# The self-attention's preparation taken batch by batch, inside the attention loops on either side of it

## The chip, the core and the metric

The kernel runs on one core of a Trainium2 chip. The time is device microseconds (us) of one launch. The core has a matrix engine (PE in the profile; its weight loads, which overlap the products, are PEld), a vector engine (DVE), a scalar engine (ACT), a general engine (POOL) and a sync engine (SP) that issues the transfers. Each engine works through its own instructions in the order in which the program gives them; between engines there are only semaphores.

## The reference

Four decoder layers on `x` of 2 batches x 256 tokens x 128 channels. The last layer is a cross attention with 16 heads of 64 over 512 context rows, and then a block whose first part is this (16 query heads, 4 key and value heads of 8 channels, causal):

```python
x = x + xattn3(layernorm(x), ctx, mask_k, ...)
h = rmsnorm(layernorm(x), ln1_w)
qkv = h @ wqkv.T
q, k, v = split(qkv)
q, k = rope(q), rope(k)
x = layernorm(x) + causal_attention(q, k, v) @ wo.T
x = x + moe(rmsnorm(x))
```

The two batches are independent of one another in all of it. What a kernel must give back is `x` after the last mixture of experts (8 experts, 2 chosen per token).

## The kernel before, in words

One launch does all layers; activations stay on the chip. The order on every engine is written out by hand: each engine has one function, in it loops with small helpers, and a helper that is called at some `n`, `step` or `part` of a loop stands there in that engine's queue.

The last cross attention (`attention3`) runs over 32 pairs `n` (two heads, one half of a batch's queries; batch 0 is n = 0 to 15). PE does the scores of pair n (`scores_pair`, L1903), VectorE the maxima (L1031), ScalarE the exponentials (L663), VectorE the scaling by the sums (`scale_pair`, L1014, one pair behind), PE the transposes (`turn_pair`, L1914, two pairs behind), ScalarE copies them (L655), and at every odd n PE multiplies half a group of four heads with the values (`values_part`, L1929). VectorE copies a finished group out (`out3`, L1020). `project3(0)` and `project3(1)` (L1966) are the output projections of the batches; both stand at the end of the loop.

Then all that the self-attention needs is prepared for both batches at once, with nothing beside it: the residual, two norms whose roots are taken on POOL (L1456 to L1475, L471 to L484), a transpose (L1571), its copy (L556), the projection to queries, keys and values (L2267), the rotation (L1489 to L1496), a split of each number into three bf16 parts (`split`, L912 to L916), their spreading into a table `REP` (`spread`, L317, one part each on POOL, ScalarE and VectorE) of 8 tiles (keys and queries of 4 token tiles), 80 transposes of it (`stack`, L1620) in 12 lots, and a copy of each lot to where the attention reads it (`stack_copy`, L302, even lots on VectorE, odd ones on ScalarE). `keep_busy` (L1989) puts 10 products whose result nobody reads into two waits of PE:

```python
keep_busy(7, 5)
turn_xn(9)
...
keep_busy(3, 7)
stack(ROPE_TILES)
stacked(pe, ROPE_TILES[-1])
```

The self-attention (`attention_self` on PE, `attention(2)` on ScalarE and VectorE) runs over 8 groups `g` of four heads (batch 0 is g = 0 to 3) in 12 steps, each of which holds four stages of different groups: the maxima of the scores of group `step` (three banks: PE L1635 to L1644, VectorE L926 and L929), their split and transpose (VectorE L996 to L1000, PE L1764), the scores again with the maxima taken off (L1660 to L1675) and the exponentials (L614) of group `step - 2`, the products with the values (L1783, L1786) of `step - 3`, and the transpose back (L1806) of `step - 4`. The mixture of experts follows (L1869, L1881).

## Time and profile before

| | us |
|---|---|
| three runs | 560.18, 559.19, 559.20 |
| median | 559.20 |
| span of the profiled execution, first to last instruction | 557.4 |
| PE busy in the span | 503.7 (90%) |
| VectorE busy | 354.4 (64%) |
| ScalarE busy | 312.1 (56%) |
| POOL busy | 62.5 (11%) |

The profiled execution has no time of its own in the list beside its span; the median lies 1.8 us above the span, and that is taken as what lies around it. A row of the profile names an instruction by engine, source line and tile: `L1914 PE ps<-const_t,Qst` is line 1914, run on PE, written to `ps` (the accumulators) from `const_t` and `Qst`. In rows of time the first number is the start in the span and the second how long the merged instructions took; what stands in brackets at the end is the idle time before them and what ended it. The granted clock of PE is given as a share of its full speed: 1.00 is 2.4 GHz and 0.50 is 1.2 GHz.

### The profile page before, as it was taken

Reading aid. Unit: us, or ns where it says so; the run is one execution under the profiler, and the core shown is the slowest. Engines: PE = TensorE matmul, PEld = TensorE weight load, DVE = VectorE, ACT = ScalarE, POOL = GpSimd, SP = SyncE. Lnnn points to the kernel's source line nnn. Section 1 sums busy time; section 2 is a strip of 40 time slices with the busy share of each in tenths; the row PEclk is TensorE's granted clock in tenths of the full one; section 3 lists DMA queues with packets and bytes.
Section 4 is the critical chain, followed back from the end, with each engine's and each line's share of the span. In section 5 each row is a group of like instructions: output and inputs, shape, how many; then the busy total and the mean of one; then the engine's idle time right before and its main releaser. Section 6 shows DMA issues by size and latency. Waiting matters only on the chain.

```text
span 557.4 us, 9259 instructions
## 1 busy us (share of the span) xinstructions
PE 503.7 (90%) x3340; PEld 308.6 (55%) x3344; DVE 354.4 (64%) x922; ACT 312.1 (56%) x537; POOL 62.5 (11%) x161
## 2 busy tenths in 40 slices
PE   5889998999979998898887699999999868988997
PEld 2334456999924444445553234555557545556987
DVE  6767746565888772496336656787773486554664
ACT  6447786463326776148357289788783043555331
POOL 4021120100011110000270000000001230000000
PEclk9889999999989999899998799999999987999999
DMA  4669301034224000000000000000000500000000
GB/s 142 198 183 405 123 4 34 2 86 132 76 74 149 1 1 1 2 0 1 1 0 1 1 0 1 1 1 2 1 2 0 228 0 1 1 2 1 2 11 10
DMA packets 11612, 26.17 MB, mean 47 GB/s; under 512 B 2128, under 2 KB 6864, under 8 KB 10928
## 3 DMA queue, kind: packets, MB, share of 16 engines
q1 hardware_dynamic: 11568, 25.59, 13.9%
q8 instruction: 27, 0.44, 0.3%
q14 instruction: 17, 0.14, 0.1%
HBM read 22.44 MB, written 3.15 MB: 46 GB/s over the span
## 4 chain that ended last, share of the span: by engine, by line
PE 75%; DVE 10%; ACT 5%; issue 4%; DMA 2%; SPq 2%; POOL 1%; DVEq 0%; ACTq 0%; POOLq 0%
PE ps L1903 6%; PE ps L1914 6%; PE ps L1929 5%; PE ps L2020 5%; PE ps L2008 5%; PE ps L1707 5%; PE ps L1791 5%; PE ps L1869 4%; PE ps L1689 4%; DVE mxs L924 3%; PE ps L1979 2%; PE ps L1881 2%; PE ps L2167 2%; PE ps L1989 2%; PE ps L1718 1%
## 5 line engine op out<-in xcount | busy, mean ns | idle before, releaser
L924 DVE TENSOR_REDUCE mxs<-ps 128x1 f32<-128x512 f32 x128 | 81.8, 682 | 23.9 <-PE ps L1707 22.5
L614 ACT ACTIVATE PR<-ps 128x1024 f32<-128x1024 f32 x80 | 77.4, 977 | 34.9 <-PE ps L1689 17.4
L1031 DVE TENSOR_REDUCE nm<-ps 128x1 f32<-128x512 f32 x64 | 41.1, 684 | 25.0 <-PE ps L1903 25.0
L1707 PE MATMUL ps<-Kst,Qst 84*128 84x512 bf16 x128 | 49.8, 398 | 6.3 <-DVE mxs L924 3.4
L655 ACT COPY PR<-ps 128x512 f32<-128x512 f32 x64 | 37.9, 596 | 16.9 <-PE ps L1914 16.9
L663 ACT ACTIVATE Qst<-ps,nm 128x512 f32<-128x512 f32 x64 | 45.5, 710 | 1.5 <-DVE nm L1031 1.3
L1689 PE MATMUL ps<-Qst,Kst 84*128 84x256 bf16 x256 | 45.8, 273 | 0.1
L1914 PEld LDWEIGHTS ps<-const_t,Qst 128*128 128x128 f32 x256 | 27.4, 140 | 24.3 <-DVE Qst L1014 11.8
L692 ACT ACTIVATE PR<-ps,cols_t 128x256 f32<-128x256 f32 x64 | 26.5, 471 | 23.4 <-PE ps L2008 23.0
L623 ACT COPY Qst<-ps 12x1024 bf16<-12x1024 bf16 x24 | 24.0, 999 | 27.6 <-PE ps L1764 27.6
L1903 PE MATMUL ps<-VX,FC 64*128 64x512 f32 x128 | 36.1, 641 | 0.1
L1914 PE MATMUL ps<-const_t,Qst 128*128 128x128 f32 x256 | 35.4, 280 | 0.9 <-ACT PR L655 0.9
L1791 PE MATMUL ps<-PR,VX 128*9 128x256 f32 x512 | 33.5, 380 | 0.0
L2020 PEld LDWEIGHTS ps<-FC,PR 128*128 128x128 f32 x256 | 30.9, 192 | 0.8
L1707 PEld LDWEIGHTS ps<-Kst,Qst 84*128 84x128 bf16 x128 | 12.7, 100 | 33.6 <-DVE mxs L924 22.6
L1689 PEld LDWEIGHTS ps<-Qst,Kst 84*128 84x128 bf16 x256 | 23.3, 97 | 14.4 <-issue 2.3
L2008 PE MATMUL ps<-parts,FC 128*128 128x256 f32 x128 | 30.4, 381 | 0.9 <-DVE scr L974 0.8
L1869 PE MATMUL ps<-scr,FC 128*128 128x256 f32 x128 | 30.6, 382 | 0.6 <-DVE scr L974 0.6
L2020 PE MATMUL ps<-FC,PR 128*128 128x128 f32 x256 | 31.0, 275 | 0.0
L1929 PE MATMUL ps<-PR,Kst 128*64 128x256 f32 x256 | 30.9, 385 | 0.0
L1014 DVE TENSOR_SCALAR Qst<-Qst,rsum 128x512 f32<-128x512 f32 x64 | 28.3, 484 | 1.1
L1989 PE MATMUL ps<-ctxT,const_t 128*128 128x512 f32 x48 | 23.6, 640 | 5.7 <-DMA const_t<-in_const 5.7
(369 smaller groups left out, 883.5 us busy)
## 6 DMA issues: line engine op xcount, KB each, us to landing
Kst<-k_rows SPq DMA_DIRECT2D x48, 96.0 KB
FC<-in_fc SPq DMA_DIRECT2D x2, 2048.0 KB, 12.0
Qst<-q_rows SPq DMA_DIRECT2D x48, 48.0 KB
FC<-in_w SPq DMA_DIRECT2D x1, 2048.0 KB, 8.7
k_rows<-REP SPq DMA_DIRECT2D x12, 128.0 KB, 2.2
REP<-in_w SPq DMA_DIRECT2D x1, 1536.0 KB, 6.8
q_rows<-REP SPq DMA_DIRECT2D x20, 64.0 KB, 2.0
FC<-in_w2e SPq DMA_DIRECT2D x1, 1024.0 KB, 10.8
```

What stands on the lines that cost most here:

```text
L614: act.activation(PRg[:, g % 2, u * 1024:u * 1024 + width], bank(3 + 2 * (n % 2), 2)[:, 0:width], ACT.Exp, scale=scale).then_inc(s.p_ready, 1)
L663: act.activation(P3[:, i % 8, :], bank(S_BANKS[n % 2][half]), ACT.Exp, bias=nm3[:, i % 8:i % 8 + 1], accum_out=sum3[:, i % 16:i % 16 + 1]) ...
L924: i = dve.tensor_reduce(m[:, u // 4, u % 4:u % 4 + 1], bank(n % 2), AX_X, ALU.max)
L1689: i = pe.matmul(bank(3 + 2 * (n % 2), 2)[:, k * SQ:(k + 1) * SQ], Kst[0:ROWS_A, b, h0 + u, k * P:(k + 1) * P], Qst[0:ROWS_A, b, h0 + u, :] ...
L1707: pe.matmul(bank(n % 2), Qst[0:ROWS_A, b, h, q0:q0 + P], Kst[0:ROWS_A, b, h, :], start=True, stop=True).then_inc(s.smax_ready, 1)
L1791: i = pe.matmul(o[32 * c:32 * c + HD + 1, :], Vaug[:, 4 * b + k, h0 + c, 0:HD + 1], pr[:, c * 1024 + k * SQ:c * 1024 + (k + 1) * SQ], star ...
L1869: i = pe.matmul(bank(2 * (n % 2) + c // 2)[:, c % 2 * SQ:(c % 2 + 1) * SQ], w13[:, e, c * P:(c + 1) * P], lnT[:, b * SQ:(b + 1) * SQ], sta ...
L1903: pe.matmul(bank(S_BANKS[n % 2][half]), Q3[d0:d0 + DH3, r, q0:q0 + P], K3[d0:d0 + DH3, r, b * SK:(b + 1) * SK], start=True, stop=True)\
L1914: ins = pe.transpose(bank(T_BANKS[half])[:, k * P:(k + 1) * P], P3[:, i % 8, k * P:(k + 1) * P], ident)
L1929: pv = pe.matmul(bank(O_BANKS[g % 2])[DH3 * c:DH3 * (c + 1), r * SQ:(r + 1) * SQ], V3[:, 4 * b + k, DH3 * (h0 + 2 * r + c):DH3 * (h0 + 2 * ...
L2008: i = pe.matmul(bank(2 * (n % 2) + c // 2)[:, c % 2 * SQ:(c % 2 + 1) * SQ], fc1[:, n % E, c * P:(c + 1) * P], hdT[:, n % 3, :], start=True ...
L2020: i = pe.matmul(bank(4 + n % 2)[:, j * P:(j + 1) * P], actT[:, n % 2, c, j * P:(j + 1) * P], fc2[:, n % E, c, :], start=(c == 0), stop=(c ...
```

## The change

The preparation is cut by batch. Batch 0's is put into the second half of `attention3` (pairs 22 to 35): its projection into bank 7 at n = 22 on PE, the residual and norms on VectorE at n = 23 to 25, transposes at 26, their copy on ScalarE at 27, the projection at 28, the rotation on VectorE at 29, the split and all spreading on POOL alone, and 40 transposes in two pieces among the last value products. Bank 7 is free for this since the groups 4 to 7 all gather their output in bank 6. Batch 1's is put into the first steps of the self-attention: its projection in step 0, the norms at the ends of steps 0 and 1 and in step 2, projection in step 2, rotation, split and a third of the spreading on VectorE at the start of step 3 (the other two thirds on POOL), and 40 transposes on PE ahead of step 4, the first step that works on batch 1's scores. `keep_busy` is gone from here. Batch 0's queries and the rotation's tables move into the storage of the values that groups 0 to 3 have used up.

The first piece is PE's queue at the end of the cross attention, before the change: L1929 are value products, L1966 the projections, L1989 `keep_busy`, L1571 and L2267 the transposes and projection, L1620 the transposes of the table, L1635 the first scores of the self-attention.

```order
L1914 MATMUL ps<-const_t,Qst 128x128 x16
L1929 MATMUL ps<-PR,Kst 64x256 x8
L1966 MATMUL ps<-wd_t,REP 128x128 x16
L1929 MATMUL ps<-PR,Kst 64x256 x16
L1966 MATMUL ps<-wd_t,scr 128x128 x16
L1989 MATMUL ps<-ctxT,const_t 128x512 x7
L1571 MATMUL ps<-const_t,xn 128x128 x4
L2267 MATMUL ps<-wd_t,scr 128x192 x4
L1989 MATMUL ps<-ctxT,const_t 128x512 x3
L1620 MATMUL ps<-identb,REP 96x128 x80
L1635 MATMUL ps<-FC,Qst 128x128
```

The same place after the change; here L1993 are the value products, L1666 the transposes of the table, L1689 and L1691 the first scores of the self-attention and their mask, L2037 the projection of batch 1, L1696 the next scores.

```order
L1978 MATMUL ps<-const_t,Qst 128x128 x16
L1993 MATMUL ps<-PR,Kst 64x256 x8
L1666 MATMUL ps<-identb,REP 96x128 x20
L1993 MATMUL ps<-PR,Kst 64x256 x8
L1666 MATMUL ps<-identb,REP 96x128 x20
L1993 MATMUL ps<-PR,Kst 64x256 x8
L1689 MATMUL ps<-FC,Kst 128x128
L1691 MATMUL ps<-maskb,identb 128x128
L2037 MATMUL ps<-wd_t,scr 128x128 x16
L1696 MATMUL ps<-FC,Kst 128x256
```

The projection of batch 0 has left this place for n = 22; the one of batch 1 has moved behind the first scores; 40 of the 80 transposes stand between the value products, and the other 40 have gone further down, ahead of step 4.

The second piece is VectorE's queue in the first steps of the self-attention, before (L926 and L929 read the maxima of a step, L996 to L1000 split them):

```order
L302 COPY Qst<-ps 96x8x128 x2
L926 TENSOR_REDUCE mxs<-ps 128x4
L929 TENSOR_REDUCE mxs<-ps 128x2 x2
L996 TENSOR_SCALAR mp<-mxs 128x2x4
L997 SCALAR_TENSOR_TENSOR mr<-mxs,mp 128x8
L999 CAST mp<-mr 128x2x4
L1000 TENSOR_TENSOR mp<-mr,mp 128x2x4
```

The same after, step 0 and the start of step 1 (L995 and L998 are the maxima, L885 to L888 `last_projected(1)`, L1076 to L1080 the split):

```order
L1100 COPY scr<-ps 128x512
L995 TENSOR_REDUCE mxs<-ps 128x4
L998 TENSOR_REDUCE mxs<-ps 128x2 x2
L885 TENSOR_TENSOR x<-x,ps 128x256
L1168 BN_STATS st<-x 128x6 x2
L1171 BN_AGGR mv<-st 128x2 x2
L888 COPY Kst<-x 128x256
L1076 TENSOR_SCALAR mp<-mxs 128x2x4
L1077 SCALAR_TENSOR_TENSOR mr<-mxs,mp 128x8
L1079 CAST mp<-mr 128x2x4
L1080 TENSOR_TENSOR mp<-mr,mp 128x2x4
```

And after, the end of step 2 and the start of step 3 (L922 and L926 end the rotation of batch 1, L981 to L985 its split, L321 the spreading):

```order
L1080 TENSOR_TENSOR mp<-mr,mp 128x2x4
L919 TENSOR_TENSOR Kst<-ps,const_t 128x160
L920 TENSOR_TENSOR Kst<-ps,const_t 128x20x4
L921 TENSOR_TENSOR Kst<-ps,const_t 128x20x4
L922 COPY FC<-ps 128x4x8
```

```order
L926 TENSOR_TENSOR Kst<-Kst 128x320
L981 CAST parts<-Kst 128x320
L982 TENSOR_TENSOR rest<-Kst,parts 128x320
L983 CAST parts<-rest 128x320
L984 TENSOR_TENSOR rest<-rest,parts 128x320
L985 CAST parts<-rest 128x320
L321 COPY REP<-parts 128x4x3x8
L321 COPY REP<-parts 128x16x24
L321 COPY REP<-parts 128x4x3x8
L321 COPY REP<-parts 128x16x24
L995 TENSOR_REDUCE mxs<-ps 128x4
```

What VectorE had done before the self-attention began now stands between the maxima of step 0 and their split, and in front of the maxima of step 3.

```diff
+        Qs4 = [Kst[:, 0, 0:8, :].rearrange("p g (a t) -> p (g a) t", a=2), Qst[:, 1, :, :]]
...
-        ROPE_TILES = range(0, 8)
+        ROPE_TILES = (range(0, 4), range(4, 8))
+        LOT_BANKS = (0, 1, 2, 3, 0, 1, 6, 0, 1, 6, 0, 1)
+        LOT_BEHIND = (None, None, None, None, 0, 1, None, None, None, 6, 7, 8)
...
+        def o3_bank(g):
+            return O_BANKS[g % 2] if g < G // 2 else O_BANKS[0]
...
-            pool.wait_ge(s.proj_ready, 4)
+            rstd_of(8, 0, of_batch(0))
+            rstd_after(9, 0, of_batch(0))
+            link(pool.memset(V4[:, :, :, :], 0.0))
+            pool.memset(V4[:, :, :, HD:HD + 1], 1.0).then_inc(s.setup_pool, 1)
             pool.memset(REP[:, :].bitcast(F32), 0.0).then_inc(s.setup_pool, 1)
-            pool.wait_ge(s.setup_pool, 4)
-            rstd_of(8)
-            rstd_after(9)
-            for n in ROPE_TILES:
-                spread(pool, n)
+            pool.wait_ge(s.setup_pool, 5)
+            pool.wait_ge(s.rope_ready, 1)
+            ropes, r = qrope[:, 0:2, :].rearrange("p t n -> p (t n)"), rest[:, 0:320]
+            link(pool.tensor_copy(parts[:, 0, 0:320], ropes))
+            link(pool.tensor_tensor(r, ropes, parts[:, 0, 0:320], ALU.subtract))
+            link(pool.tensor_copy(parts[:, 1, 0:320], r))
+            link(pool.tensor_tensor(r, r, parts[:, 1, 0:320], ALU.subtract))
+            link(pool.tensor_copy(parts[:, 2, 0:320], r))
+            for n in ROPE_TILES[0]:
+                for j in range(NPART):
+                    i = spread(pool, n, j)
+                    if j < NPART - 1:
+                        link(i)
+                i.then_inc(s.rep_first, 1)
+            rstd_of(8, 1, of_batch(1))
+            rstd_after(9, 1, of_batch(1))
+            for n in ROPE_TILES[1]:
+                for j in range(2):
+                    pool.wait_ge(s.parts_ready, j + 1)
+                    if j == 0:
+                        pool.wait_ge(s.rep_turned, lots_till[n - 4])
+                    spread(pool, n, j).then_inc(s.rep_pool, 1)
...
+            def rms1_out(b, at):
+                act.wait_ge(s.xn_turned, TURNS.index((9, b)) + 1)
+                act.activation(rms1T[b], at[:, 0:SQ], ACT.Copy, scale=CB["rms1"]).then_inc(s.lnT_ready, 1)
...
+                    if a == 2 and step == G // 2:
+                        stack_lots(act, ROPE_TILES[1])
...
+                        if a == 2 and step == 2 and part == 0:
+                            rms1_out(1, bank(6))
...
+                    if n == 27:
+                        rms1_out(0, bank(7))
...
-            ln_out(9)
-            act.wait_ge(s.setup_pool, 4)
-            spread_and_stack(act, ROPE_TILES, ROPE_TILES)
+            stack_lots(act, ROPE_TILES[0])
...
+            def last_projected(b, at):
+                dve.wait_ge(s.proj_ready, 4 + b)
+                link(dve.tensor_tensor(x[:, of_batch(b), :], x[:, of_batch(b), :],
+                                       at[:, 0:SQ].rearrange("p (t n) -> p t n", t=2), ALU.add))
+                batch_variances(b)
+                link(dve.tensor_copy(kept[:, b * SQ:(b + 1) * SQ].rearrange("p (t n) -> p t n", t=2),
+                                     x[:, of_batch(b), :]))
+            def last_normalised(b):
+                dve.wait_ge(s.rstd_ready, norm(8, b) + 1)
+                for t in (2 * b, 2 * b + 1):
+                    i = dve.tensor_scalar(x[:, t, :], x[:, t, :], mv[:, t, 0:1], rstd[:, t:t + 1],
+                                          ALU.subtract, ALU.mult)
+                signal_xn(i, norm(8, b) + 1)
+            def last_scaled(b):
+                dve.wait_ge(s.rstd_ready, norm(9, b) + 1)
+                for t in (2 * b, 2 * b + 1):
+                    i = dve.tensor_scalar(xn[:, t, :], x[:, t, :], rstd[:, NT + t:NT + t + 1], None, ALU.mult)
+                i.then_inc(s.xn_ready, 1)
+            def ropes(b, at):
+                dve.wait_ge(s.qkv_ready, b + 1)
...
+                q2 = qrope[:, 2 * b:2 * b + 2, :]
+                signal(dve.tensor_tensor(q2, q2, qrot[:, 2 * b:2 * b + 2, :], ALU.add), 'rope_ready')
+            def last_spreads():
+                split(qrope[:, 2:4, :].rearrange("p t n -> p (t n)"), 320, 320)
+                for n in ROPE_TILES[1]:
+                    dve.wait_ge(s.rep_turned, lots_till[n - 4])
+                    spread(dve, n, 2).then_inc(s.rep_dve, 1)
...
+                    if a == 2 and step == 3:
+                        ropes(1, bank(6))
+                        last_spreads()
+                    if a == 2 and step == G // 2:
+                        stack_lots(dve, ROPE_TILES[1])
...
+                        if a == 2 and step == 0 and part == 7:
+                            last_projected(1, bank(6))
+                        if a == 2 and step == 1 and part == 7:
+                            last_normalised(1)
+                        if a == 2 and step == 2 and part == 1:
+                            last_scaled(1)
...
-                for n in range(PAIRS3 + PV3 + 4):
+                for n in range(4 * G + PV3 + 1):
+                    g, part = divmod(n - PV3 - 4, 4)
+                    if 0 <= g < G and part == 0:
+                        out3(g)
                     if n < PAIRS3:
                         for half in range(2):
                             i = 2 * n + half
                                               negate=True).then_inc(s.nm3_ready, 1)
                     if 0 <= n - 1 < PAIRS3:
                         scale_pair(n - 1)
-                    g, part = divmod(n - PV3 - 4, 4)
-                    if 0 <= g < G and part == 0:
-                        out3(g)
+                    if n == 23:
+                        last_projected(0, bank(7))
+                    if n == 24:
+                        last_normalised(0)
+                    if n == 25:
+                        last_scaled(0)
+                    if n == 29:
+                        dve.wait_ge(s.setup_pool, 5)
+                        ropes(0, bank(7))
+                    if n == PAIRS3 + 3:
+                        stack_lots(dve, ROPE_TILES[0])
...
-                    for spread_by in (s.rep_dve, s.rep_act, s.rep_pool):
-                        pe.wait_ge(spread_by, tl + 1)
-                    if n >= 4:
-                        pe.wait_ge(s.stack_act if n % 2 else s.stack_dve, (n - 4) // 2 + 1)
+                    if tl < 4:
+                        pe.wait_ge(s.rep_first, tl + 1)
+                    else:
+                        pe.wait_ge(s.rep_pool, 2 * (tl - 4) + 2)
+                        pe.wait_ge(s.rep_dve, tl - 4 + 1)
+                    behind = LOT_BEHIND[n]
+                    if behind is not None:
+                        pe.wait_ge(s.stack_act if behind % 2 else s.stack_dve, behind // 2 + 1)
...
+            def qkv(b, at):
+                pe.wait_ge(s.lnT_ready, rows_copied(9, b))
+                for j in range(2):
+                    i = pe.matmul(at[:, 192 * j:192 * (j + 1)], rms1T[b][:, j * P:(j + 1) * P],
+                                  WD["wqkv"], start=True, stop=True)
+                i.then_inc(s.qkv_ready, 1)
...
+                    if step == G // 2:
+                        pe.wait_ge(s.smax_read, MAXB[a] + 3 * step)
+                        stack(ROPE_TILES[1])
+                        stacked(pe, ROPE_TILES[1][-1])
                     for part in range(4):
                         if step < G:
                             scores_max(a, step, part)
+                        if step == 0 and part == 1:
+                            project3(1)
+                        if step == 2 and part == 0:
+                            turn_rows(9, 1, bank(6))
+                        if step == 2 and part == 3:
+                            qkv(1, bank(6))
...
-                            pe.wait_ge(s.o3_ready, g - 1)
+                            pe.wait_ge(s.o3_ready, g if g > G // 2 else g - 1)
...
-                    if n == PAIRS3 + LAG:
-                        project3(0)
                     if n >= PV3 and (n - PV3) % 2:
                         values_part(*divmod(n - PV3 - 1, 4))
                         values_part(*divmod(n - PV3, 4))
+                    if n == 22:
+                        project3(0)
+                    if n == 26:
+                        turn_rows(9, 0, bank(7))
+                    if n == 28:
+                        qkv(0, bank(7))
+                    if n == PAIRS3 + 1:
+                        stack(ROPE_TILES[0][0:2])
+                    if n == PAIRS3 + 3:
+                        stack(ROPE_TILES[0][2:4])
...
-                pe.wait_ge(s.p3_ready, 2 * PAIRS3 - 2)
                 pe.wait_ge(s.o3_ready, G // 2 * (b + 1))
                 for t in (2 * b, 2 * b + 1):
                     for r in range(8):
-                        i = pe.matmul(bank(1 - b)[:, t % 2 * P:(t % 2 + 1) * P],
+                        i = pe.matmul(bank(7 - b)[:, t % 2 * P:(t % 2 + 1) * P],
...
-            project3(1)
-            keep_busy(7, 5)
-            turn_xn(9)
-            pe.wait_ge(s.lnT_ready, 10)
...
-            keep_busy(3, 7)
-            stack(ROPE_TILES)
-            stacked(pe, ROPE_TILES[-1])
+            stacked(pe, ROPE_TILES[0][-1])
```

## Rows read from the trace of the kernel before

**Rows 1.** Busy us of each engine by stretch; PEclk is the granted clock.
```profile
345.00:420.00 75.00, 74.92 (x498) 41.67 (x500) 57.01 (x129) 59.39 (x150) 0.00 (x0) 1.00 0.01 1
...
437.00:462.50 25.50, 18.45 (x112) 12.44 (x110) 16.72 (x60) 8.22 (x15) 7.47 (x14) 0.87 0.18 73
462.50:477.90 15.40, 13.82 (x114) 8.48 (x114) 10.53 (x28) 6.51 (x8) 0.00 (x0) 0.78 0.01 1
```
**Rows 2.** Timeline: PE where the cross attention ends; first transposes back.
```profile
424.83 3.84 PE L1966 MATMUL ps<-wd_t,REP 128*128 128x128 f32 x32
428.60 3.67 PE L1929 MATMUL ps<-PR,Kst 128*64 128x256 f32 x32
...
433.16 3.81 PE L1966 MATMUL ps<-wd_t,scr 128*128 128x128 f32 x32 [0.89 <-DVE scr L1020]
...
477.95 0.41 PE L1806 MATMUL ps<-const_t,scr 128*128 128x128 f32 x2 [0.64 <-issue]
```
**Rows 3.** Timeline of the cross attention: VectorE, and PE's transposes of a pair.
```profile
403.40 1.29 DVE L1031 TENSOR_REDUCE nm<-ps 128x1 f32<-128x512 f32 x2 [1.61 <-PE ps L1903]
...
405.59 0.68 DVE L1020 COPY scr<-ps 128x512 f32<-128x512 f32 x1
...
410.88 0.88 DVE L1014 TENSOR_SCALAR Qst<-Qst,rsum 128x512 f32<-128x512 f32 x2
...
411.46 1.13 PE L1914 MATMUL ps<-const_t,Qst 128*128 128x128 f32 x8
...
413.06 0.88 DVE L1014 TENSOR_SCALAR Qst<-Qst,rsum 128x512 f32<-128x512 f32 x2
```
**Rows 4.** Timeline of the preparation: VectorE.
```profile
437.00 0.42 DVE L1456 TENSOR_TENSOR x<-x,ps 128x256 f32<-128x256 f32 x1 [3.15 <-PE ps L1966]
...
438.28 0.39 DVE L1470 COPY scr<-x 128x512 f32<-128x512 f32 x1
...
439.98 1.12 DVE L862 TENSOR_SCALAR x<-x,mv,rstd 128x128 f32<-128x128 f32 x4 [1.31 <-POOL rstd L472]
...
445.41 0.33 DVE L1489 TENSOR_TENSOR PR<-ps,const_t 128x160 f32<-128x160 f32 x1 [1.76 <-PE ps L2267]
...
447.31 0.33 DVE L912 CAST parts<-PR 128x320 bf16<-128x320 f32 x1
...
449.73 0.70 DVE L317 COPY REP<-parts 128x96 bf16<-128x96 bf16 x4
```
**Rows 5.** Timeline of the preparation: PE.
```profile
444.45 1.57 PE L2267 MATMUL ps<-wd_t,scr 128*128 128x192 f32 x8 [0.78 <-ACT scr L556]
...
450.05 1.54 PE L1620 MATMUL ps<-identb,REP 128*96 128x128 bf16 x24 [1.46 <-DVE REP L317]
...
455.26 6.14 PE L1620 MATMUL ps<-identb,REP 128*96 128x128 bf16 x56 [3.67 <-DVE FC L302]
```
**Rows 6.** Groups of POOL by form: busy us, mean ns, idle before.
```profile
L317 POOL COPY REP<-parts 128x384 bf16<-128x384 bf16 x4 | 2.5, 615 | 3.0 <-PE ps L1620 3.0
...
L524 POOL TENSOR_SCALAR PR<-PR 128x352 f32<-128x352 f32 x1 | 1.4, 1395 | 0.1
```
**Rows 7.** Timeline of POOL in the preparation.
```profile
447.70 2.25 POOL L317 COPY REP<-parts 128x96 bf16<-128x96 bf16 x4 [5.72 <-DVE parts L912]
...
457.31 0.51 POOL L317 COPY REP<-parts 128x384 bf16<-128x384 bf16 x1 [3.03 <-PE ps L1620]
```
**Rows 8.** Busy us by stretch, around a fall of the clock.
```profile
450.90:454.30 3.40, 0.69 (x13) 0.54 (x10) 3.19 (x12) 1.83 (x4) 1.66 (x3) 1.00 0.00 0
454.30:461.10 6.80, 5.84 (x55) 5.87 (x56) 4.02 (x11) 3.43 (x6) 0.51 (x1) 0.51 0.01 2
```
**Rows 9.** Timeline of the self-attention's start: PE, VectorE, ScalarE.
```profile
461.44 1.01 ACT L302 COPY Qst<-ps 96x1024 bf16<-96x1024 bf16 x1 [1.08 <-PE ps L1620]
...
463.82 1.38 DVE L929 TENSOR_REDUCE mxs<-ps 128x2 f32<-128x512 f32 x2
465.23 0.17 DVE L996 TENSOR_SCALAR mp<-mxs 128x8 bf16<-128x8 f32 x1
...
468.41 0.64 PE L1660 MATMUL ps<-Qst,FC 96*128 96x512 bf16 x1
...
470.54 0.42 PE L1642 MATMUL ps<-FC,Qst 96*128 96x256 bf16 x1
...
470.79 1.02 ACT L614 ACTIVATE PR<-ps 128x1024 f32<-128x1024 f32 x1 [3.26 <-PE ps L1665]
```

More of the change, by code:

```diff
@@ L316, in spread, with stack_lots @@
                 .to_broadcast([P, heads, 3, HD])
-            i = eng.copy(to, src) if eng is nc.scalar else eng.tensor_copy(to, src)
-            i.then_inc(done, 1)
-        def spread_and_stack(eng, to_spread, to_stack):
+            return eng.tensor_copy(to, src)
+        def stack_lots(eng, tile_range):
             odd, done = (1, s.stack_act) if eng is nc.scalar else (0, s.stack_dve)
-            def stack_lots(tile):
-                for n, (tl, h0, nh) in enumerate(lots):
-                    if tl == tile and n % 2 == odd:
-                        eng.wait_ge(s.rep_turned, n + 1)
-                        stack_copy(eng, n, tl, h0, nh).then_inc(done, 1)
-            behind = list(to_stack)
-            for n in to_spread:
-                spread(eng, n)
-                while behind and behind[0] <= n - 2:
-                    stack_lots(behind.pop(0))
-            for tile in behind:
-                stack_lots(tile)
+            for n, (tl, h0, nh) in enumerate(lots):
+                if tl in tile_range and n % 2 == odd:
+                    eng.wait_ge(s.rep_turned, n + 1)
+                    stack_copy(eng, n, tl, h0, nh).then_inc(done, 1)
         MROW0 = [0, 0, PAD]
@@ L1501, in _ @@
-            spread_and_stack(dve, ROPE_TILES[4:8], ROPE_TILES)
             def route_logits(b):
```

142 lines of the change are left out of this document (51 added, 91 removed).

## The prediction

> **What bounds the kernel now.** I read the shares of busy time first: PE 90% against 64% for VectorE, so PE sets the time wherever it is full. Then the busy time by stretch, to see where it is full. In the cross attention it is: 74.92 of 75.00 us at full clock, with VectorE at 57.01 and ScalarE at 59.39 [rows 1]. In the preparation it is not: 18.45 of 25.50 us at a mean clock of 0.87, and 6.17 of those were `keep_busy`; and in the first steps of the self-attention PE is busy 13.82 of 15.40 us, but at 0.78 of its clock [rows 1]. Last the timeline of both stretches: PE waits there for VectorE (3.67 us ahead of the last 56 transposes, 1.46 ahead of the first 24 [rows 5]), which works through a chain (residual, norm, norm, rotation, split, spread) with PE, POOL and ScalarE as links [rows 4].
>
> The part that the change touches runs from the end of the last but one group's value products (424.83) to the first transpose back (477.95 [rows 2]): 53.1 us, low stretches of the clock included. The profiled execution took 557.4 us by its span; the median is 559.2, so 1.8 lies around the span. I rebuild these 53.1 us for the new order, with what is put into the loop added.
>
> **The change part by part.** At full clock:
>
> 1. Into the loop. `project3(0)` moves, 3.84 [rows 2] wherever it stands. Two transposes of batch 0 at 0.14 each (8 in 1.13 [rows 3]) are 0.3, its projection is half of 1.57 [rows 5]: 0.8. PE is full there, so all of it counts. VectorE's insertions count where they delay PE. The smallest rows hide: between reduces VectorE idles 1.61 in a pair [rows 3], and the residual with its statistics (437.00 to 438.67, less half a copy for half the tokens: 1.4), the normalising (half of 1.12) and the scaling (0.6 at most) [rows 4] fit in it. The rotation does not: 445.41 to 447.31, 1.9 [rows 4], and `out3` with 0.68 [rows 3] now stands ahead of the reduces. 1.9 + 0.6 less 1.61 and less the 0.14 by which the scaling ends (410.88 + 0.44) before its transposes start at 411.46 leaves 0.8 late. Together 5.7 (4.9 if the delay is caught up; 7.0 if neither gap can be used).
> 2. 40 transposes of batch 0, 0.055 each (1.54 for 24 less the start-up [rows 5]): 2.2, and the last group's values 3.67 [rows 2]: 5.9.
> 3. The wait for `out3` (0.89) and `project3(1)` (3.81) [rows 2]: 4.7. The first scores go ahead of it.
> 4. From there VectorE has what the preparation had, now in the middle of the maxima: 0.5 for scores, five reads at 0.69 (two in 1.38 [rows 9]) 3.4, residual and statistics 1.4, two splits of maxima 1.4 (465.23 to 465.93 each [rows 9]), two half sets of scalings 1.1 [rows 4], and 0.5 for semaphores. That is 8.3, with PE mostly idle. What is queued behind the waiting VectorE is the split of step 0's maxima, for which PE's mask transposes and ScalarE's copy wait in turn.
> 5. Step 2 up to the projection of batch 1: transposes 0.3, the exponentials' products (468.41 to 470.54 at half clock [rows 9], so 1.1), ScalarE's exponential 1.02 [rows 9] ahead of its copy of half the 0.78 [rows 5] (0.4), some scores 0.5, projection 0.8: 4.1. The copy waits on ScalarE for PE, and the next mask copy and exponentials queue behind it.
> 6. VectorE's rotation, split and spreads of batch 1, 445.41 to 450.43: 5.0 [rows 4]. They stand ahead of step 3's maxima, so every stage behind waits; with a maxima read (0.69) and what is left of a split (0.5) 6.2. A third of the spreads, the split and the rotation were on this path before; the two thirds of the spreading that POOL does are eight at 0.56 (four in 2.25 [rows 7]), 4.5 beside VectorE's split and spreads, so hidden.
> 7. What is left of step 3 on PE: one set of exponentials' products at full clock and a third of one: 1.4.
> 8. 40 transposes of batch 1 ahead of step 4: 2.2, and the later of their 6 lots wait for a copy before them out of three banks, on ScalarE 1.01 each [rows 9]: 3.9 (2.2 if no copy is waited for, 4.2 if two on ScalarE are).
>
> The sum is 5.7 + 5.9 + 4.7 + 8.3 + 4.1 + 6.2 + 1.4 + 3.9 = 40.2, against 53.1: 12.9 saved.
>
> The clock takes some back. PE's clock fell to its lower level (0.51, which is 1.2 GHz) for 6.80 us after PE had been busy 0.69 of 3.40 us [rows 8]. Of before's two such stretches in the interval the new order keeps the cause: parts 4 and 6 leave PE idle for several us, with no `keep_busy` between. So I expect two stretches of some 6.8 us; full of work one costs half, 3.4, and with VectorE's chain in it as little as nothing. I take 2.0 and 1.8, the middle: 12.9 - 3.8 = 9.1 saved, and 557.4 - 9.1 + 1.8 = 550.0 us (rounded).
>
> POOL's new chain has to hide. Its five split operations on 320 columns have no row of before: the nearest are 1.40 (352 columns of 32 bits, one input [rows 6]) and 0.51 (384 columns of 16 bits [rows 7]). I take 0.7, nearer to the second, since three of the five write bf16. 3.5 + twelve spreads at 0.56 [rows 7] 6.7 + 17 links at 0.08 (estimate from the gaps between spreads) 1.4 = 11.6. The rotation stands behind the scalings at 413.06 [rows 3] and ends 0.9 + 1.9 later, at 415.9; PE comes to the last tile's transposes at 424.83 + 1.1 (20 transposes) + 1.84 (half the last values) + 0.2 (4 more) + 0.8 (the delay of part 1) = 428.8, 12.9 later: hidden by 1.3. With 1.40 for each split operation and 0.615 for a spread [rows 6] it is 15.8, and PE waits 2.9.
>
> The row has POOL's spread at 0.56 beside a working VectorE and 0.51 alone [rows 7]. The Trainium skill (GPSIMD Engine Reference, § 3.1 Elementwise, side-by-side cycle accounting) speaks against the move of the two subtractions: it has POOL at about half VectorE's rate for two inputs, 4497 ns for 2048 columns, an estimate of 0.7 us for 320; with 0.7 the sum would stay as it is, by the upper row it loses the 2.9.
>
> The loads of the experts' weights that wait for the end of the cross attention start some 4 us later and are wanted first 40 us behind: hidden. The clearing of the table and of the values moves onto a POOL that is idle in the loop (0.00 of 75 [rows 1]).
>
> **The rivals.** *The clock holds* (0.25): one low stretch, or two that lie beside VectorE's chain and cost 1.0 in all. For it: PE has work put between part 4 and 6. Against: the 0.69 of 3.40 that came before the fall. 557.4 - 11.9 + 1.8 = 547.3.
>
> *POOL's split is slow* (0.12): 1.40 each as above; PE waits 2.9 ahead of the last transposes and a low clock of 1.1 more follows: 554.0.
>
> *POOL is held up by VectorE, and the kernel is slower* (0.08). VectorE is busy 57 of 75 us in the loop [rows 1], and no row shows a POOL copy beside its scaling. If POOL's operations take f times as long, batch 0 is late by 10.2f - 11.5 and batch 1 by 4.5f - 6.3 (its spreads against the 5.0 of part 6 and the first 24 transposes): 14.7f - 17.8 in all. It decides at f = 1.8; at f = 2 the loss is 11.6 and the time 561.6, 2.4 slower than before. Against it stand the 0.56 and 0.51 of rows 7.
> The Trainium skill has such a rule (GPSIMD Engine Reference, § 1 Specifications): POOL shares its SBUF interfaces with VectorE and contends with instructions that use both ports or two SBUF inputs. By that rule the spreads beside the split of VectorE should have suffered too, and the trace's 10% does not agree with a factor of 2.
>
> *VectorE becomes the bound of the loop* (0.07): it works 57 of 75 us, and if each of the ten pairs from n = 23 on comes 0.8 late, 8 of the 9.1 are lost: 558.2. Against: its idle 1.61 comes in each pair [rows 3].
>
> **How the numbers follow.** The forecast has 0.48, with a range of its own of 547.5 to 552.5 (clock 1.4 to 6.3 in place of 3.8, and part 1 from 4.9 to 7.0). The range goes from 546.5 (the clock holds, and the transposes' copies hide) to 555.0 (slow split): 0.85 of the cases less their edges. A measurement of this kernel tells 0.2%, 1.1 us, from no change. Faster: the first three cases, 0.85, and one in seven of the last, 0.86. Same: the rest of the last, 0.06. Slower: 0.08.
>
> **What the profile after would show.** Right: the value products of the last groups run on with transposes between them without a wait for POOL; the first scores of the self-attention come some 12 us after the start of the last group; PE's idle time ends on VectorE's maxima in steps 0, 1 and 3, in all about 12 us; two stretches of PEclk near 0.5 between step 1 and step 4; from the second half of the self-attention on, every row is as before, 9 us earlier. Wrong: idle PE ahead of the 40 transposes ended by POOL; in pairs 23 to 33 idle PE ended by VectorE on more than one or two pairs; steps 4 and later at other intervals than before; a wait for the experts' weights; or a chain of waits that runs through POOL in step 3.

## The result, and the profile after

The changed kernel took 551.78, 549.03, 553.14 and 553.74 us, median 552.5, beside 559.2 for the kernel before: a ratio of 0.9871, 95% interval 0.9834 to 0.9909. A second set on another occasion gave a median of 552.5 in five executions (a sixth took 1782 us and is left out) and 0.9872 (0.9816 to 0.9928); the medians by themselves differ by 6.7 us in the first set and by 5.2 in the second (557.7 before). The forecast was 550.0 in 546.5 to 555.0, faster. The profiled execution of the changed kernel has a span of 549.9 us, against 557.4.

PE's timeline at the end of the cross attention and in the first steps, after. The lines are the answer to [rows 2, 5]; line numbers are those of the changed kernel (L1978 the transposes of a pair, L1666 those of the table, L1993 the value products, L1689 the first scores, L2037 the projection of batch 1, L1818 the transposes of the maxima, L1620 those of batch 1, L1674 its projection, L1860 the first transpose back).

```profile
410.67 1.09 PE L1978 MATMUL ps<-const_t,Qst 128*128 128x128 f32 x8 [0.80 <-DVE Qst L1094]
...
424.70 1.24 PE L1978 MATMUL ps<-const_t,Qst 128*128 128x128 f32 x8 [1.23 <-DVE Qst L1094]
...
429.18 1.12 PE L1978 MATMUL ps<-const_t,Qst 128*128 128x128 f32 x8 [0.33 <-ACT PR L678]
...
432.10 1.32 PE L1666 MATMUL ps<-identb,REP 128*96 128x128 bf16 x20
433.35 1.95 PE L1993 MATMUL ps<-PR,Kst 128*64 128x256 f32 x16
435.23 1.32 PE L1666 MATMUL ps<-identb,REP 128*96 128x128 bf16 x20
...
438.35 0.23 PE L1689 MATMUL ps<-FC,Kst 96*128 96x128 bf16 x1
...
439.21 3.84 PE L2037 MATMUL ps<-wd_t,scr 128*128 128x128 f32 x32 [0.22 <-DVE scr L1100]
442.89 0.27 PE L1696 MATMUL ps<-FC,Kst 96*128 96x256 bf16 x1
...
446.92 0.28 PE L1818 MATMUL ps<-identb,mp 128*12 128x128 bf16 x2 [1.63 <-DVE mp L1080]
...
450.53 0.69 PE L1620 MATMUL ps<-const_t,xn 128*128 128x128 f32 x2 [2.50 <-DVE xn L903]
...
455.68 0.92 PE L1674 MATMUL ps<-wd_t,scr 128*128 128x192 f32 x4 [0.19 <-ACT scr L576]
456.43 0.38 PE L1724 MATMUL ps<-Kst,FC 96*128 96x512 bf16 x1
...
462.82 0.37 PE L1696 MATMUL ps<-FC,Kst 96*128 96x256 bf16 x1 [2.77 <-DVE mxs L995]
...
465.41 3.93 PE L1666 MATMUL ps<-identb,REP 128*96 128x128 bf16 x40
470.49 0.41 PE L1860 MATMUL ps<-const_t,scr 128*128 128x128 f32 x2 [1.15 <-DVE Qst L311]
```

The preparation's own stretch of 25.5 us [rows 1] is gone. What is left of its waits for VectorE stands in the steps: 1.63, 2.50 and 2.77 us, one each in steps 1, 2 and 3, where the forecast had named steps 0, 1 and 3. (From 440 to 472 us PE is busy 23.0 of 32.0 us, so it idles 9.0, where the forecast said about 12.) The value products run on with transposes between them, and no wait of PE in this stretch ends on POOL.

The busy time by stretch of the same kernel (length, then PE, PEld, DVE, ACT, POOL, and the granted clock), as in [rows 1, 8]:

```profile
345.00:420.00 75.00, 73.56 (x499) 42.88 (x498) 57.44 (x132) 55.95 (x141) 5.81 (x9) 1.00 0.01 1
447.99:454.80 6.81, 4.31 (x24) 2.92 (x24) 3.03 (x11) 0.80 (x2) 0.65 (x1) 0.50 0.01 2
454.80:461.80 7.00, 5.06 (x47) 3.12 (x46) 6.54 (x23) 4.45 (x6) 2.27 (x4) 0.99 0.00 0
461.80:468.60 6.80, 5.78 (x48) 4.41 (x49) 3.95 (x11) 2.33 (x4) 1.51 (x5) 0.51 0.00 0
```

Two stretches of 6.8 us at the lower level (1.2 GHz), each beginning in one of the long waits above, with full clock between them. And PE, which had been full in the cross attention (74.92 of 75.00), is now at 73.56: 0.53 of that is a wait for ScalarE that the kernel before has as well, just ahead of 345.00; most of the rest is the wait of 0.80 above, which is new.

**The interval that is compared below.** The first value products of the cross attention start between 344.2 and 348.6 us, differing from trace to trace of kernels that have the same instructions up to there, and from the first transpose back in step 4 to the end every trace has 79.4 us. So each trace is read from its first value products to that transpose, in two parts: the cross attention (to the end of its last value products) and the rest.

| trace | cross attention | from there to the first transpose back | sum |
|---|---|---|---|
| before, two traces | 86.63, 86.59 | 45.68, 44.31 | 132.31, 130.90 |
| after, two traces | 92.27, 92.27 | 32.07, 32.86 | 124.34, 125.13 |

### The profile page after: what moved, and what is told of

It is laid out like the page before. It is cut to its first block, busy times and chain, and to the rows that moved or that the text cites. A ratio compares the mean times of both kernels' runs of the same rounds, so it can differ in the third digit from the quotient of the medians.

```text
span 549.9 us, 9205 instructions
## 1 busy us (share of the span) xinstructions
PE 491.1 (89%) x3320; PEld 302.8 (55%) x3324; DVE 354.1 (64%) x912; ACT 309.8 (56%) x530; POOL 72.7 (13%) x186
## 4 chain that ended last, share of the span: by engine, by line
PE 71%; DVE 14%; issue 5%; ACT 5%; SPq 2%; DMA 2%; POOL 1%; DVEq 0%; ACTq 0%; POOLq 0%
PE ps L2091 5%; PE ps L2079 5%; PE ps L1761 5%; PE ps L1967 5%; PE ps L1978 5%; PE ps L1845 5%; PE ps L1993 5%; PE ps L1933 4%; PE ps L1743 4%; DVE mxs L993 3%; PE ps L2050 2%; PE ps L1945 2%; PE ps L1860 1%; PE ps L1772 1%; PE ps L2037 1%
## 5 line engine op out<-in xcount | busy, mean ns | idle before, releaser
L468 POOL TENSOR_SCALAR ve<-mv 128x2 f32<-128x2 f32 (+1 forms) x13 | 3.0, 233 | 306.5 <-DVE mv L1171 169.3
L1978 PEld LDWEIGHTS ps<-const_t,Qst 128*128 128x128 f32 x256 | 27.5, 140 | 26.6 <-DVE Qst L1094 14.4
L1978 PE MATMUL ps<-const_t,Qst 128*128 128x128 f32 x256 | 35.4, 280 | 3.0 <-DVE Qst L1094 2.0
L646 ACT COPY Qst<-ps 12x1024 bf16<-12x1024 bf16 x20 | 20.0, 999 | 23.6 <-PE ps L1818 23.6
L1094 DVE TENSOR_SCALAR Qst<-Qst,rsum 128x512 f32<-128x512 f32 x64 | 30.6, 520 | 1.1
L1993 PE MATMUL ps<-PR,Kst 128*64 128x256 f32 x256 | 31.2, 385 | 0.0
```

The source lines that it names most:

```text
L1978: ins = pe.transpose(bank(T_BANKS[half])[:, k * P:(k + 1) * P], P3[:, i % 8, k * P:(k + 1) * P], ident)
L1993: pv = pe.matmul(bank(o3_bank(g))[DH3 * c:DH3 * (c + 1), r * SQ:(r + 1) * SQ], V3[:, 4 * b + k, DH3 * (h0 + 2 * r + c):DH3 * (h0 + 2 * r + ...
```

## The experiments

**The same kernel again.**

> The changed kernel once more, without an edit, to see how its time spreads: its four runs lay between 549.0 and 553.7 us, those of the kernel before within 1.0. Theory (the two low stretches of PE's clock come at another place from run to run, since PE idles for several us where VectorE prepares batch 1): again a spread of 3 to 5 us, median 550 to 553. Rival (the first runs were disturbed): a spread under 1.5 us. In its trace two stretches of 6.8 us at the lower clock between the first scores and the first transpose back.

The five runs lay between 548.15 and 553.0, as the theory has it. But the kernel before, measured beside it, now spread too (556.6 to 565.1 in 17 runs), so the low stretches that are new in the changed kernel are not shown to be the cause. Its two traces differ by 0.8 us in the steps, where the first low stretch fell later in the second; what the other runs differ by has no trace, and the start of the cross attention alone moves by up to 4.4 us from trace to trace. A second trace of the kernel before:

> The kernel before once more, for a second trace of its interval from the first value products to the first transpose back (132.31 us in the first). Theory (the interval depends on where the low clock falls in the preparation, as in the changed kernel): 130 to 133.5, differing from the first by over 0.5. Rival (fixed): 132.2 to 132.4.

132.31 became 130.90 us. In the two traces the mean clock of the preparation and of the first steps was 0.84 and 0.78, then 0.92 and 0.89; it is the clock that differs. So the 53.1 us of the forecast are one trace's. First the first trace, then the second:

```profile
441.00:462.50 21.50, 14.46 (x103) 10.73 (x101) 14.11 (x49) 8.22 (x15) 5.40 (x9) 0.84 0.03 10
462.50:477.90 15.40, 13.82 (x114) 8.48 (x114) 10.53 (x28) 6.51 (x8) 0.00 (x0) 0.78 0.01 1
```

```profile
441.30:463.90 22.60, 15.51 (x109) 10.61 (x108) 15.11 (x52) 8.12 (x15) 7.21 (x13) 0.92 0.12 49
463.90:479.00 15.10, 12.69 (x114) 7.73 (x115) 10.55 (x28) 6.51 (x8) 0.00 (x0) 0.89 0.00 1
```

**Is the low clock worth what was taken for it?** Unread products in PE's three waits, first too many:

```diff
+                            keep_busy(5, 7)
                             turn_rows(9, 1, bank(6))
...
+                        if step == 1 and part == 2:
+                            keep_busy(3, 7)
...
+                        if step == 3 and part == 2:
+                            pe.wait_ge(s.rope_ready, 2)
+                            keep_busy(6, 6)
```

> Products whose result nobody reads are put into PE's three waits for VectorE: three in step 1 ahead of the transposes of the maxima, five in step 2 ahead of the transposes of batch 1, six in step 3 behind the transposes of the maxima. Theory (the low clock costs what the forecast took, 3.8 us): no low stretch there, the projection of batch 1 about 1.8 us earlier against the first scores, step 4's first transpose back 3 to 4 us earlier, time 3 to 4 us below the changed kernel of the same call. Rival (VectorE's chain sets the time of these steps, so a faster PE only waits longer): under 1 us. Second rival: the products run past the end of the waits and cost up to 1 us.

The time stayed (552.1 us, ratio to before 0.9889, 0.9840 to 0.9938). But this does not speak for the rival: the clock was at 1.00 throughout, and the products (L2066) simply ran too long, twice what I had reckoned for one. It is the second rival's case, and dearer than it had it: from the first score to the first transpose back this trace takes 33.10 us, where the changed kernel takes 32.14 and 32.93, so all that the clock gave was lost again.

```profile
444.41 2.79 PE L2066 MATMUL ps<-ctxT,const_t 128*128 128x512 f32 x6
447.69 4.51 PE L2066 MATMUL ps<-ctxT,const_t 128*128 128x512 f32 x10
459.75 5.42 PE L2066 MATMUL ps<-ctxT,const_t 128*128 128x512 f32 x12
```

Three calls show as six products and take 2.79 us where PE had waited 1.63. With 4, 5 and 5 products of half the width in the same places:

> The same three places as in the run with 3, 5 and 6 unread products, where each took 0.88 us, twice what was reckoned, and ran 0.9, 1.7 and 2.3 us past the end of VectorE's work. Now 4, 5 and 5 products of half the width (0.44 each by that run): 1.8, 2.2 and 2.2 us, inside the waits of 1.8, 2.6 and 2.4. Theory (low clock costs what the forecast took): no low stretch, no wait ended by these products, the first score to the first transpose back of step 4 in 28.0 to 29.2 us against 32.1 and 32.9 in the two traces of the changed kernel; time 3 to 4.5 us below it. Rival (VectorE's chain sets the time): 31.5 or more there.

```profile
443.40:451.00 7.60, 6.62 (x46) 4.90 (x44) 6.71 (x23) 1.00 (x1) 2.28 (x6) 1.00 0.58 246
451.00:458.70 7.70, 7.21 (x69) 4.84 (x69) 5.80 (x20) 4.01 (x5) 0.75 (x2) 1.00 0.01 2
458.70:461.20 2.50, 2.40 (x11) 1.79 (x10) 2.43 (x8) 1.00 (x1) 2.50 (x6) 1.00 0.00 0
461.20:467.00 5.80, 4.10 (x59) 3.28 (x60) 3.56 (x9) 3.36 (x5) 0.53 (x2) 1.00 0.00 0
```

548.2 us, ratio 0.9806 (0.9783 to 0.9828). From the first score to the first transpose back 28.24 us against 32.14 and 32.93: the two stretches cost 3.9 and 4.7 us, where the forecast took 3.8. VectorE's chain by itself does not set the time of these steps while the clock is low.

**How much is batch 1's move worth?** Its preparation ahead of the self-attention, batch 0's left in the loop (PE's part; the calls on the other engines move likewise):

```diff
             attention3()
+            project3(1)
             stacked(pe, ROPE_TILES[0][-1])
+            turn_rows(9, 1, bank(6))
+            qkv(1, bank(6))
+            stack(ROPE_TILES[1])
+            stacked(pe, ROPE_TILES[1][-1])
```

> Batch 1's preparation is taken out of the self-attention's steps and put ahead of them, with nothing beside it; batch 0's stays inside the cross attention. Theory: from the end of the cross attention's values the chain of batch 1 is the projection 3.9, residual 1.3, roots on POOL 2.8, scaling, transposes, copy and projection 2.4, rotation 1.9, split 2.2, spreads 0.6, transposes 3.5 and copies 1.0, some 20 us, and then the first four steps as before the change 15.4, so 35 to 36 against 32.1 in the changed kernel: 3 to 4 us slower than it, and still 3 to 5 faster than the kernel before, which is what batch 0 alone is worth. Rival (what batch 1's work hides in the steps it takes from them again, so only batch 0's move counts): within 1 us of the changed kernel.

> The kernel with batch 1's preparation ahead of the self-attention once more. Its interval was 129.97 us in the trace, 2.3 below the kernel before, while its times were level with it (ratio 1.0009). Theory (the traced run was its fastest, and the low clock falls worse in the others): an interval of 131 to 133. Rival (the interval is fixed and the difference lies ahead of it): 129.9 to 130.1, with times again level because its early stages are slower.

558.7 and 558.6 us, ratios to before 1.0009 (0.9993 to 1.0025) and 0.9993 (0.9964 to 1.0022): with batch 0 alone moved the times show no gain, and the changed kernel is 6 us faster than this one. I had expected 3 to 5 for batch 0 alone; that is refuted. The chain of one batch is shorter than that of two, but by less than half: from the end of the values to the first score it takes 22.15 and 21.92 us, for both batches it took 30.28 and 29.16, and the cross attention pays 5.6 of the difference. PE's waits in it (the last line is cut off by its view; all 40 transposes take 4.11):

```profile
438.83 3.84 PE L2020 MATMUL ps<-wd_t,scr 128*128 128x128 f32 x32 [0.79 <-DVE scr L1087]
447.48 0.66 PE L1613 MATMUL ps<-const_t,xn 128*128 128x128 f32 x2 [4.81 <-DVE xn L901]
...
454.94 3.34 PE L1659 MATMUL ps<-identb,REP 128*96 128x128 bf16 x28 [4.59 <-DVE REP L321]
```

Part of those 22 us is the clock. Like the changed kernel, this one has no `keep_busy`; its stretch from the last values to the first score has a mean clock of 0.69 (0.77 in the second trace), where the kernel before has 0.89 and 0.94, and the 40 transposes that take 4.11 here take 2.43 at full clock in a kernel further down:

```profile
438.04:460.19 22.15, 10.25 (x78) 8.98 (x79) 9.80 (x32) 3.07 (x4) 6.10 (x14) 0.69 0.37 142
```

What batch 0's move is worth with unread products in these waits was not run, so the missing gain is shown for the move without them only.

The interval of this kernel, 129.97 and 129.74, is 0.9 to 2.6 shorter than that of the kernel before, which the times don't show. It did stay fixed, near the rival's value, but its early stages are not slower: it starts at 345.78 and 347.15, the kernel before at 345.64 and 348.11. What the record does show is that both traces of the kernel before are of its longer executions: they took 559.2 (by the span and the 1.8 around it) and 560.4 us, at a mean clock of 0.966 and 0.972 over the whole execution, while its executions with 0.978 and more took 555.0 to 558.5. How long the interval is in those has no trace.

**What makes PE wait in the cross attention?** In the changed kernel VectorE's timeline around pair 25 (L1094 the scaling, L895 and L903 the norms of batch 0, L1100 the copy-out):

```profile
402.80 0.88 DVE L1094 TENSOR_SCALAR Qst<-Qst,rsum 128x512 f32<-128x512 f32 x2
403.60 0.89 DVE L895 TENSOR_SCALAR x<-x,mv,rstd 128x128 f32<-128x128 f32 x2
404.52 1.29 DVE L1114 TENSOR_REDUCE nm<-ps 128x1 f32<-128x512 f32 x2
405.73 0.15 DVE L1090 RECIPROCAL rsum<-sum 128x2 f32<-128x2 f32 x1
405.92 1.91 DVE L1094 TENSOR_SCALAR Qst<-Qst,rsum 128x512 f32<-128x512 f32 x2
```

Beside the second scaling POOL clears the table:

```profile
404.50 2.66 POOL L538 MEMSET REP<- 128x3072 f32 x1
```

Of the two operations in the 1.91 us the first took 1.52 and ended 0.28 after the clearing (407.16), the second, behind it, took 0.47. POOL clearing only the padding:

```diff
-            pool.memset(REP[:, :].bitcast(F32), 0.0).then_inc(s.setup_pool, 1)
+            pool.memset(REP[:, :].bitcast(F32).rearrange("p (n c) -> p n c", c=48)[:, :, 36:48], 0.0)\
+                .then_inc(s.setup_pool, 1)
```

> POOL clears only the quarter of the table that the spreads do not write (the padding), in place of all of it. In the changed kernel the scaling beside this clearing took 1.91 us for two where 0.88 is usual, and PE waited 0.80 for it at the next pair. Theory (POOL and VectorE hold each other up): the clearing takes about 0.7 in place of 2.66, the scaling 0.9 to 1.2, PE's wait of 0.80 goes, and the end of the cross attention comes 0.6 to 1.0 us earlier. Rival (the wait is from the scaling of batch 0's norm and the copy-out that stand ahead of the reduces): the scaling is slow as before or PE waits as long as before, time the same.

```profile
406.92 0.74 POOL L538 MEMSET REP<- 128x768 f32 x1
```

```profile
408.33 0.88 DVE L1095 TENSOR_SCALAR Qst<-Qst,rsum 128x512 f32<-128x512 f32 x2
```

The smaller clearing is over (407.66) before the scaling begins. The scaling is back at 0.88, PE's wait of 0.80 is gone, and the cross attention takes 91.24 against 92.27: 1.03 us, in the trace. The time alone (551.8, 0.9867, 0.9822 to 0.9912) could not have told. The same by itself, in pairs where the changed kernel has no POOL at all:

```diff
+            spare = parts[:, :, :].rearrange("p i n -> p (i n)").bitcast(F32)
+            pool.wait_ge(s.p3_ready, 16)
+            for _ in range(12):
+                link(pool.memset(spare[:, 0:960], 0.0))
+            pool.wait_ge(s.p3_ready, 32)
+            for _ in range(16):
+                link(pool.tensor_copy(spare[:, 480:960], spare[:, 0:480]))
```

> POOL is given work that nobody needs in the first half of the cross attention: 12 clearings of 960 numbers from pair 8 on, and 16 copies of 480 numbers from pair 16 on; nothing else is changed. Theory (the scaling on VectorE, from SBUF to SBUF, is slowed by POOL's work, the reduces out of the accumulators are not): the scaling of two takes 1.3 to 1.9 beside the clearings and beside the copies, against 0.88; a pair on VectorE then needs 1.3 + 0.15 + 1.6 = 3.05 us against PE's 3.04, so PE waits 0 to 0.5 per pair, 1 to 4 us in all, over the eight to ten pairs. Rival (the slow scalings of the changed kernel had another cause): 0.9 throughout, and the time from the first value products to the last stays at 92.3.

VectorE first beside the clearings, then beside the copies, then alone (L1101 is the scaling here):

```profile
349.99 2.12 DVE L1101 TENSOR_SCALAR Qst<-Qst,rsum 128x512 f32<-128x512 f32 x2
352.04 1.27 DVE L1121 TENSOR_REDUCE nm<-ps 128x1 f32<-128x512 f32 x2
...
376.67 1.51 DVE L1101 TENSOR_SCALAR Qst<-Qst,rsum 128x512 f32<-128x512 f32 x2
378.10 1.27 DVE L1121 TENSOR_REDUCE nm<-ps 128x1 f32<-128x512 f32 x2
...
389.54 0.88 DVE L1101 TENSOR_SCALAR Qst<-Qst,rsum 128x512 f32<-128x512 f32 x2
```

Three pairs have their scaling beside the clearings (1.89 to 2.25 in place of 0.88) and three beside the copies (1.21 to 1.51); the reduces stay at 1.27, and the cross attention takes 95.35: 3.1 us longer. This kernel and the one with the doubled split below ran once each, so they are read by their traces alone.

**Rotation and split.** The rotation one pair later (`n == 30` for `n == 29`):

> Batch 0's rotation on VectorE one pair later (n = 30), where the copy-out of a group does not follow it. In the changed kernel PE waited 1.23 for the scaling behind rotation and copy-out. Theory (rotation, copy-out and the scaling beside POOL's split add up at one pair): the wait falls to under 0.6, the end of the cross attention comes 0.5 to 1.2 earlier (91.1 to 91.8 us from the first value products to the last, against 92.27), POOL's spreads end 3 us later and the transposes do not wait, or under 0.5 for them. Rival (the wait moves with the rotation): the same 92.2 to 92.4.

92.21 against 92.27, and PE now waits 1.04 and 0.28 for the scalings behind it: the wait moved with the rotation, the rival's result (552.9 us, 0.9889, 0.9864 to 0.9915). POOL's split done twice:

> POOL does the five operations of batch 0's split twice, 3.0 us more on its chain. In the changed kernel its spreads end at 430.7 and PE starts the first 20 transposes at 432.1, for which only the first half of the spreads is needed, and the second 20 at 435.2. Theory (the chain is hidden with 1.3 us to spare at its tightest place): PE waits 0 to 0.5 ahead of the transposes, time within 1 us. Rival (POOL is on the path): 3 us longer to the end of the cross attention.

```profile
428.14 0.53 POOL L547 CAST parts<-rest 128x320 bf16<-128x320 f32 x1
428.73 5.14 POOL L321 COPY REP<-parts 128x96 bf16<-128x96 bf16 x12
```

POOL ends at 433.87, PE starts the second 20 transposes at 435.43 without a wait, and the cross attention takes 92.28. So POOL's chain has over 3 us of cover, where the forecast had 1.3.

**Together.** The half products and the smaller clearing; and then, of batch 1's lots, the last three in banks 3, 4 and 6:

```diff
-        LOT_BANKS = (0, 1, 2, 3, 0, 1, 6, 0, 1, 6, 0, 1)
-        LOT_BEHIND = (None, None, None, None, 0, 1, None, None, None, 6, 7, 8)
+        LOT_BANKS = (0, 1, 2, 3, 0, 1, 6, 0, 1, 3, 4, 6)
+        LOT_BEHIND = (None, None, None, None, 0, 1, None, None, None, None, None, 6)
...
+                        pe.wait_ge(s.p_ready, UNIT[a] + 3)
                         stack(ROPE_TILES[1])
```

(The added wait keeps these transposes off banks 3 and 4 until ScalarE's exponentials have read them.)

> Both edits that gained, together: the 4, 5 and 5 half products in PE's three waits (28.24 us from the first score to the first transpose back, against 32.1 and 32.9), and the clearing of the padding alone (91.24 us over the value products of the cross attention, against 92.27). Theory (they lie in different stages and add up): 91.2 and 28.2, 119.4 from the first value products to the first transpose back, 13 below the kernel before, time about 2.3% below it and 1.0 below the kernel with the half products alone. Rival (what the clearing gives is taken back by a clock that falls elsewhere): 120.4 or more.

> As best2, and the last three lots of batch 1's transposes go to banks 3, 4 and 6 in place of 6, 0 and 1, so that only one of them has a copy ahead of it. Theory (the forecast's term for these 40 transposes, 3.9, is 2.2 of work and the rest waits for copies): PE's wait of 0.52 between the transposes goes, that behind them (1.15 for the last copy) stays, 0.4 to 0.6 us less than best2. Rival (the copies themselves are the bound, one of 1.01 after another on ScalarE): the wait comes behind the transposes instead, within 0.2 of best2.

The first: 91.23 and 28.24 us, sum 119.40; 546.6 us, ratio 0.9783 (0.9756 to 0.9809). The second: 27.54, sum 118.70, 546.1 us, 0.9765 (0.9741 to 0.9789), the lowest median here. The 0.70 between the two stands in the traces, 0.1 more than the theory had; the times do not tell them apart. The 40 transposes of the second run through, and the 1.15 behind them stays:

```profile
461.90 2.43 PE L1667 MATMUL ps<-identb,REP 128*96 128x128 bf16 x40
465.48 0.41 PE L1861 MATMUL ps<-const_t,scr 128*128 128x128 f32 x2 [1.15 <-DVE Qst L311]
```

## Why the prediction was right, step by step

The terms against the first trace of the changed kernel, in us:

| part of the forecast | forecast | measured | read as |
|---|---|---|---|
| 1, into the loop | 5.7 | 6.8 | 432.10 - 346.15 less 424.83 - 345.64 |
| 2, batch 0's transposes, last values | 5.9 | 6.3 | 432.10 to 438.35 |
| 3, wait and `project3(1)` | 4.7 | 4.5 | to 442.89 |
| 4, VectorE to the scaling | 8.3 | 7.6 | to 450.47 |
| 5, to the projection, with one low stretch | 4.1 + 2.0 | 6.0 | to 456.43 |
| 6, VectorE's rotation to the maxima | 6.2 | 6.8 | to 463.27 |
| 7 and 8, with the other | 1.4 + 3.9 + 1.8 | 7.2 | to 470.49 |
| sum | 44.0 | 45.2 | 8.0 saved of 53.1 |

The mechanism was right in each part, and so was the case that was given the largest chance: two low stretches, which the filled waits show to be worth 3.9 to 4.7 us against 3.8 taken. The forecast's 9.1 us became 8.0 in the interval of these two traces; over all four pairs of a trace before and a trace after it is 5.8 to 8.0, and the 132.31 that the forecast started from is the longer of the two of the kernel before. This trace's run (551.8) lost another 0.5 by which its first value products came late; why the others of the first set took up to 553.7 no trace shows. The number alone would not have told the cases apart: 552.5 stands at the upper end of the forecast's own 547.5 to 552.5, and the slow split's 554.0 is nearer to it than 550.0. The traces do: POOL's split took 3.0 us, PE waited for it nowhere, and two low stretches are there.

The one term that was mis-sized by a cause I had not seen is part 1. I put the clearing of the table down as free because POOL is idle in the loop. It was not POOL's time that it cost: beside it VectorE's scaling took 1.91 for 0.88, and 1.03 of the cross attention went with it. Where I did look for a delay by VectorE, at the rotation, I found it (0.8 forecast; PE's wait behind it is 1.23), in part for the same reason, since POOL's split starts as soon as the rotation ends, beside the next scaling, which took 1.69. The wait of 0.33 that follows ends on ScalarE and stands in the kernel before as well (0.33 at 421.90). So part 1 has two waits for VectorE, 2.03 us in place of 0.8, within what the forecast allowed (one or two pairs); what is left, 4.7, is PE's own work, reckoned at 4.9. Part 6 is 0.6 over; 0.4 of that is VectorE's four spreads, 1.10 us beside POOL's spreads, where the row that the forecast used has 0.70.

POOL's and VectorE's lines for this, and the ends of parts 4 (L903) and 6 (L998), from the changed kernel:

```profile
422.19 0.79 POOL L543 TENSOR_TENSOR rest<-Kst,parts 128x320 f32<-128x320 f32 x1
423.54 1.69 DVE L1094 TENSOR_SCALAR Qst<-Qst,rsum 128x512 f32<-128x512 f32 x2
425.02 5.65 POOL L321 COPY REP<-parts 128x96 bf16<-128x96 bf16 x12
...
450.00 0.47 DVE L903 TENSOR_SCALAR xn<-x,rstd 128x128 f32<-128x128 f32 x2
...
460.97 1.10 DVE L321 COPY REP<-parts 128x96 bf16<-128x96 bf16 x4
...
462.60 0.67 DVE L998 TENSOR_REDUCE mxs<-ps 128x2 f32<-128x512 f32 x1
```

That rival which made the kernel slower had the contention mostly the wrong way round. POOL was held up little: its split took 0.45 to 0.79 per operation, 3.0 in all against 3.5, its twelve spreads 5.65 against 6.7, and the doubled split cost nothing. Some 0.5 of the 5.65 go with VectorE's scalings, since the same twelve took 5.14 and 5.07 in the two runs in which they came later and mostly behind the last scalings: a factor of 1.1, where the rival needed 1.8. VectorE loses most. The slow split (1.40 each) fell with the same lines. The rival in which VectorE becomes the bound of the whole loop did not occur, but `pool_beside` shows how it would: with POOL at work beside six scalings the loop is 3 us longer.

The Trainium skill says (GPSIMD Engine Reference, § 1 Specifications) that POOL's SBUF interfaces are shared with VectorE, with contention for VectorE's instructions in a mode that uses two ports or with two inputs from SBUF. The runs agree that there is contention for the scaling, which goes from SBUF to SBUF (2.12 and 1.51 for 0.88), and show the reduces, which read the accumulators, untouched at 1.27; in which mode VectorE ran the scaling no trace shows. The Trainium skill also has POOL at about half VectorE's rate for two inputs (GPSIMD Engine Reference, § 3.1 Elementwise, side-by-side cycle accounting). The estimate of 0.7 us from its figure was near the 0.79 measured; the ratio is smaller here, since VectorE's same subtraction of 320 columns took 0.49.

What I had not asked is what each half of the change is worth. Batch 0's move alone, without `keep_busy`, shows nothing in the times: the preparation is a chain, one batch still takes 22 of its 30 us, part of that at the lower clock, and the cross attention takes 5.6 more.

Four smaller things in the forecast's working do not come out. With neither gap used, part 1 is 4.9 + 2.5 = 7.4 and not 7.0, and the range of the forecast's own case would end 0.4 higher. The rival with VectorE as the bound comes to 558.0 or 558.1 by its own terms, not 558.2. The sign that the first scores come some 12 us after the start of the last group does not fit part 2 of the forecast, which has 5.9 us there; the trace has 6.3. And the 1.3 us of cover for POOL were over 3.

## What to carry to other kernels

Work moved into another loop must be priced on the engine beside it too: an idle engine is no free one if its work slows an engine that has little to spare, as the clearing on POOL slowed VectorE's scaling here. A chain of which half the work is moved away keeps more than half its length (22 of 30 us here), so price the chain that is left and what the other place pays. And where waits in the middle of a stage let PE's clock fall, fill them only up to the end of the wait: here the right filling gave 4 us, twice as much of it nothing.

## What the runs showed of the hardware

VectorE's 128x512 scaling from SBUF to SBUF took 0.88 us for two alone, 1.89 to 2.25 beside clearings on POOL (1.91 in the changed kernel), 1.21 to 1.51 beside copies of 480 numbers on POOL. POOL's twelve spreads took 5.65 us beside VectorE's scalings and 5.14 and 5.07 mostly behind them. And the start of the cross attention moved by up to 4.4 us between traces of kernels alike up to there (344.15 to 348.57), so that 1 us in a later stage was only to be seen inside one stage: over the cross attention, traces of kernels alike in it agreed to 0.03 us (92.25 to 92.28).
